# One product for delta's first factor, B and C; some elementwise work moved to GpSimd; a new job order

## The chip, the cores and the metric

The kernel runs on one core of one Trainium2 chip. The metric is the device time of one execution in microseconds (us). A core has five engines with queues of their own: TensorE (PE, matrix products and transposes; PEld is its weight load), VectorE (DVE), ScalarE (ACT), GpSimd (POOL) and SyncE (SP, which issues the DMAs here). Each works off its instructions in program order and waits on semaphores.

## The reference

A block of three parts on a stream x of 4 x 1024 tokens with 512 channels: a feed-forward layer with ternary weights, a selective state-space layer (Mamba), and the same feed-forward layer again.

```python
def step(h, inp):                       # N = 16 states per channel
    d_l, B_l, C_l, x_l = inp
    h = h * exp(d_l[:, :, None] * A) + (d_l * x_l)[:, :, None] * B_l[:, None, :]
    return h, einsum('ben,bn->be', h, C_l)

def ffn(x):                             # wu, wg, wd: ternary(W), 512 <-> 2048
    return (silu(x @ wu.T) * (x @ wg.T)) @ wd.T

def mamba(r):                           # E = 1024 channels inside
    rn = rmsnorm(r) * norm_w
    skip, x_in = rn @ W_skip, rn @ W_in
    x = silu(causal_conv4(x_in, conv_w) + conv_b)          # depthwise, 4 taps
    delta = softplus(x @ W_delta_1 @ W_delta_2 + b_delta_2) # 1024 -> 128 -> 1024
    y = scan(step, delta, x @ W_B, x @ W_C, x)
    return r + ((y + x * W_D) * silu(skip)) @ W_out

x = x + 0.5 * ffn(layernorm(x))
x = x + mamba(layernorm(x))
x = x + 0.5 * ffn(layernorm(x))
```

## The kernel before, in words

The 4096 tokens are cut into 16 chunks of 256. Everything is pipelined by hand over the chunks: while chunk i is scanned, chunk i+1 goes through the first feed-forward layer and the projections before the scan, and chunk i-1 through the output projection and the second feed-forward layer. The phases are "fill", "first", 14 times "loop", "last" and "drain".

A phase has 32 slots. Each slot holds one step of the scan (one of the 16 states, for one half of the 1024 channels) on all engines:

- POOL writes u times B into a ring of four buffers `h` (L647, 128x1024) and adds the state carried over (L651). It works three steps ahead of the transposes (`U_AHEAD`).
- ACT makes the decay exp(delta A) in PSUM (L880), two steps ahead.
- DVE runs the scan over the 256 tokens (L1164, two instructions for a step).
- PE transposes the states into PSUM (L1377, `states_T`, the last thing in its slot). It waits until DVE has added up the step before (`y_added`).
- DVE multiplies the transposed states by C and adds them up in `y` (L1190, `y_add`; L1187 for the first state of a half).

So in each slot DVE's `y_add` must be done before PE's transposes of that slot, and these before DVE's `y_add` of the next slot. PE and DVE can't drift apart by more than about a slot.

Between these stand the jobs, in the order of a table written out by hand, `LOOP_SLOTS` (L88): U and G are the up and gate products of the feed-forward layers for 256 hidden channels (U1, G1 first layer, U2, G2 second), DN the down products, T and Tp transposes of normalised rows, SK and IN the projections of the Mamba layer by quarters of the channels, D1 delta's first factor, BC the product for B and C, BT its transpose for B, D2_q delta's second factor, YT_q the transpose of y back, OM the output projection. ("OM_0", 0, 4) is parts 0 to 3 of a job. A job writes to one of four PSUM banks, and a later job waits until the other engines have used the bank's content (`bank_used`). The same table gives the slot in which ACT, DVE and POOL treat a result: a job that is not the last of its slot in that slot, the last one in the next.

What the change touches: `hidden_gate` (L1200, DVE: gate product times the activated up product, 16 in a chunk), `gated` (L1250, DVE: y + x D, and then times the skip gate `gz`), `conv` (L1222, DVE: three of the four taps, six instructions for a quarter), `delta_1` (L1443), `b_and_c` (L1450), `b_T` (L1467), and their readers on ACT (L934, L938, L981). Of `x_times_d` (L753, POOL), `mask_history` (L1215, DVE) and `mask_carry` (L1166, DVE) it moves only the slot. `first_state` (L653, POOL) stands in slot 6 of a chunk for the second half of the channels and waits for `mask_carry`, which DVE has in slot 8.

Of the kernel before, what the change touches and what calls it, by code (L numbers as in the profile page):

```python
# [21 lines left out]
P = 128  # L22
D, E, F, N, DD = 512, 1024, 2048, 16, 128
B, L = 4, 1024
TAPS = 4
TOK = B * L
CH = 256
# [5 lines left out]
CONV_STEPS = (TAPS - 1) * 2 - 1  # L33
# [23 lines left out]
def planes_of(s):  # L57
# [26 lines left out]
    ["D1", "BC"],  # L84
    ["BT", "D2_0", "D2_1"],
# [3 lines left out]
    ["T1_0", "T1_1", ("OM_0", 0, 4)],  # L89
    ["U1_0", "G1_0"],  # L90
    ["U1_1", "G1_1"],
    ["U1_2", "G1_2"],
    ["U1_3", "G1_3", "YT_2"],
    ["YT_3", "U1_4", "G1_4"],
    ["U1_5", ("OM_0", 4, 5), "G1_5", "U1_6"],
    [("OM_0", 5, 8), "G1_6"],
    [("DN1_0", 0, 3), ("OM_1", 0, 8)],
    ["U1_7", "G1_7"],
    [("DN1_1", 0, 1), ("DN1_0", 3, 9), ("DN1_1", 1, 2)],
    [("DN1_0", 9, 14)],  # L100
    ["T2_0", ("DN1_0", 14, 16), ("DN1_1", 2, 5)],
    [("DN1_1", 5, 12), ("SK_0", 0, 1), "T2_1"],
    [("DN1_1", 12, 16), ("SK_0", 1, 2), ("SK_1", 0, 2)],
    [("SK_2", 0, 2)],
    [("SK_3", 0, 1), "U2_0"],
    [("SK_3", 1, 2), "Tp_1"],
    ["Tp_0", "G2_0"],
    [("IN_2", 0, 2)],
    [("IN_3", 0, 2), ("IN_0", 0, 1), "U2_1"],
    ["YT_0", "YT_1", "G2_1", ("IN_0", 1, 2)],  # L110
    ["U2_2", "G2_2", ("IN_1", 0, 2)],
    ["U2_3", "G2_3", "U2_4"],
# [35 lines left out]
    ["D1"],  # L148
    ["BC", "D2_0", "D2_1"],
    ["BT", "D2_2", "D2_3"],  # L150
# [42 lines left out]
NEXT = {"T1_0", "T1_1", "DN1_0", "DN1_1", "Tp_0", "Tp_1", "IN_0", "IN_1", "IN_2", "IN_3", "D1", "BC", "BT", "D2_0", "D2_1", "D2_2", "D2_3"} | UG[1]  # L193
# [7 lines left out]
for _ph, _has in PHASES.items():  # L201
# [6 lines left out]
    assert set(ORDER[_ph]) == _has and len(SLOTS[_ph]) == STEPS  # L208
NBANK = 4
# [4 lines left out]
XD_0 = 2  # L214
XD_1 = 8
NEXT_LN = 29
MASK_1 = 8
MASK_0 = 24
MASK_H = 0
# [14 lines left out]
def step_of(ph, i, p):  # L234
# [61 lines left out]

def job_no(ph, i, name):
# [48 lines left out]
def macaron_kernel(nc, resid, norm_w, W_skip, W_in, conv_w, conv_b, W_delta_1, W_delta_2, b_delta_2, W_B, W_C,  # L346
# [10 lines left out]
    with ctx:  # L357
# [81 lines left out]
        y = sb("y", [P, TB, HE * P])  # L439

# [10 lines left out]
        wd1_loaded, wd2_loaded, wbc_loaded = sem("wd1_loaded"), sem("wd2_loaded"), sem("wbc_loaded")  # L451
# [57 lines left out]
        def _(sp):  # L509
# [98 lines left out]
        def _(pool):  # L608
# [118 lines left out]
            def add_edges(ph, i, half):  # L727
# [34 lines left out]
            def run(ph, i):  # L762
# [4 lines left out]
                for s in range(STEPS):  # L767
# [8 lines left out]
                    if after(ph, "OM_1", 0, s):  # L776
                        rstd(ph, i, "2")
                    for kind, p in hidden_units(ph, s):
                        hidden_low(ph, i, kind, p)
# [24 lines left out]
        def _(sc):  # L804
# [110 lines left out]
            def conv_in(ph, i, q):  # L915
# [673 lines left out]
```

## Time and profile before

| | us |
|---|---|
| median of 3 runs | 3043.34 (3043.31 to 3052.29) |
| the profiled execution | 3045.95 |
| its span, first to last instruction | 3044.2 |
| PE busy | 2796.4 (92%) |
| DVE busy | 2709.3 (89%) |
| POOL busy | 1993.6 (65%) |
| ACT busy | 1809.8 (59%) |

A busy time is the union of an engine's instructions. Matmuls overlap in their pipeline, so the pace of PE is read from the starts of successive ones, or from the chain of waits, whose pieces don't overlap. Of the waits of the engines, those count that end last before the chain goes on; most of ACT's and POOL's waits cost nothing.

### The profile page before, as it was taken

How to read it: one execution, taken by the hardware profiler on the slowest of the kernel's cores; microseconds unless marked ns; L12 is line 12 of the kernel's file. 1: busy time of each engine (PE TensorE's matmuls, PEld its weight loads, DVE VectorE, ACT ScalarE, POOL GpSimd, SP SyncE). 2: the span in 40 equal slices, each digit the busy share in tenths (PEclk: the TensorE clock that was granted, in tenths of full speed). 3: DMA queues.
4: the chain of work that ended last, by engine and by line, in shares of the span. 5: the costliest groups of instructions: out<-in, count | busy, mean ns of one | idle time of the engine just before them, and what ended most of it. 6: DMA issues, size and time to landing. Idle time of an engine off the chain costs nothing.

```text
span 3044.2 us, 53491 instructions
## 1 busy us (share of the span) xinstructions
PE 2796.4 (92%) x18791; PEld 2192.2 (72%) x18791; DVE 2709.3 (89%) x3613; ACT 1809.8 (59%) x4212; POOL 1993.6 (65%) x1875
## 2 busy tenths in 40 slices
PE   4777899999999999999999999999999999999888
PEld 3556677776877777787777768777777877777655
DVE  6359898999999999998999899999999989999992
ACT  6255656565565656556565655656565565656551
POOL 2165676757677675767777576776757677775761
PEclk9888899999999999999999999999999999999888
DMA  6010101001010100101010010101001010100100
GB/s 252 28 32 18 32 22 36 18 22 43 15 39 22 36 18 22 43 17 37 21 36 18 22 43 15 39 22 36 18 22 43 17 38 22 36 18 22 35 29 8
DMA packets 53313, 99.88 MB, mean 33 GB/s; under 512 B 7804, under 2 KB 9144, under 8 KB 52536
## 3 DMA queue, kind: packets, MB, share of 16 engines
q1 hardware_dynamic: 53048, 96.45, 10.1%
q8 instruction: 153, 2.51, 0.3%
q14 instruction: 112, 0.92, 0.1%
HBM read 87.78 MB, written 8.65 MB: 32 GB/s over the span
## 4 chain that ended last, share of the span: by engine, by line
PE 64%; DVE 20%; issue 6%; ACT 3%; POOL 1%; DVEq 0%; ACTq 0%; POOLq 0%
PE ps L1415 17%; PE ps L1426 14%; PE ps L1438 11%; PE ps L1377 10%; DVE h L1164 8%; PE ps L1491 6%; DVE y L1190 4%; DVE xc L1233 2%; PE ps L1447 2%; PE ps L1454 2%; PE ps L1464 2%; DVE act L1206 1%; DVE act L1198 1%; DVE xw L1256 1%; ACT ps L880 1%
## 5 line engine op out<-in xcount | busy, mean ns | idle before, releaser
L647 POOL TENSOR_TENSOR h<-u,bb 128x1024 f32<-128x1024 f32 x512 | 1222.1, 2387 | 305.5 <-PE ps L1377 298.4
L880 ACT ACTIVATE ps<-delta,a_neg 128x255 f32<-128x255 f32 x2048 | 882.4, 466 | 664.1 <-DVE h L1164 662.2
L1164 DVE TENSOR_TENSOR_SCAN h<-ps,h 128x512 f32<-128x512 f32 x1024 | 1191.8, 1205 | 33.3 <-POOL h L651 17.6
L1190 DVE SCALAR_TENSOR_TENSOR y<-ps,ccur,y 128x512 f32<-128x512 f32 x960 | 670.3, 739 | 46.9 <-PE ps L1377 45.9
L1377 PE MATMUL ps<-ident,h 128*128 128x128 f32 x4096 | 564.1, 280 | 97.4 <-DVE y L1190 93.2
L1377 PEld LDWEIGHTS ps<-ident,h 128*128 128x128 f32 x4096 | 475.7, 144 | 183.8 <-issue 80.4
L1415 PE MATMUL ps<-xh,q_gate 128*128 128x256 f16 x2048 | 462.4, 273 | 37.5 <-DVE act L1198 22.6
L1415 PE MATMUL ps<-xh,q_up 128*128 128x256 f16 x2048 | 466.6, 275 | 15.9 <-DVE xl L1103 12.9
L1415 PE MATMUL ps<-xl,q_up 128*128 128x256 f16 x2048 | 466.7, 275 | 0.0
L1415 PE MATMUL ps<-xl,q_gate 128*128 128x256 f16 x2048 | 462.1, 273 | 0.0
L742 POOL TENSOR_TENSOR hl<-act,hh 128x512 f16<-128x512 f32 x256 | 300.9, 1178 | 233.5 <-ACT hh L905 233.5
L1426 PE MATMUL ps<-q_down,hh 128*128 128x512 fp8e4 x1024 | 388.9, 380 | 3.1 <-issue 2.8
L1426 PE MATMUL ps<-q_down,hl 128*128 128x512 fp8e4 x1024 | 388.7, 380 | 0.0
L900 ACT ACTIVATE act<-ps,tanh_sc 128x512 f32<-128x512 f32 x256 | 173.3, 677 | 192.6 <-PE ps L1415 125.7
L1415 PEld LDWEIGHTS ps<-xh,q_gate 128*128 128x128 fp8e4 x2048 | 200.6, 98 | 77.2 <-issue 53.5
L1198 DVE SCALAR_TENSOR_TENSOR act<-act,ps 128x512 f32<-128x512 f32 x256 | 173.0, 676 | 82.8 <-ACT act L900 82.8
L1438 PE MATMUL ps<-xrT,w_in 128*128 128x256 f32 x1024 | 234.6, 383 | 1.1 <-ACT xrT L911 1.1
L1415 PEld LDWEIGHTS ps<-xh,q_up 128*128 128x128 fp8e4 x2048 | 201.5, 98 | 47.4 <-issue 19.4
L1491 PE MATMUL ps<-w_out,gz 128*128 128x512 f32 x512 | 234.7, 603 | 0.7 <-DVE gz L1259 0.7
L1438 PE MATMUL ps<-xrT,w_skip 128*128 128x256 f32 x1024 | 233.9, 379 | 0.0
L1415 PEld LDWEIGHTS ps<-xl,q_gate 128*128 128x128 fp8e4 x2048 | 200.6, 98 | 35.1 <-issue 9.3
L1415 PEld LDWEIGHTS ps<-xl,q_up 128*128 128x128 fp8e4 x2048 | 201.7, 98 | 31.6
(133 smaller groups left out, 3449.4 us busy)
## 6 DMA issues: line engine op xcount, KB each, us to landing
bb<-b_scratch SPq DMA_DIRECT2D x224, 256.0 KB, 3.2
xs<-in_L_attn_resid_dram SPq DMA_DIRECT2D x17, 512.0 KB, 3.8
out_dram<-xs SPq DMA_DIRECT2D x16, 512.0 KB, 4.3
wraw<-in_L_ffn_W_up_dram SPq DMA_DIRECT2D x4, 1024.0 KB, 8.9
wraw<-in_L_ffn_W_gate_dram SPq DMA_DIRECT2D x4, 1024.0 KB, 13.1
wraw<-in_L_ffn_W_down_dram SPq DMA_DIRECT2D x4, 1024.0 KB, 14.2
w_in<-in_L_attn_W_in_dram SPq DMA_DIRECT2D x1, 2048.0 KB, 21.6
w_skip<-in_L_attn_W_skip_dram SPq DMA_DIRECT2D x1, 2048.0 KB, 8.8
```

Source lines behind the costliest of these rows:

```text
L647: pl.tensor_tensor(h[:, s % RING, :, :], u[:, :, :], bb[:, planes_of(s) % 2, s % PLANES:s % PLANES + 1, :].broadcast_to([P, HE, CH]), ALU. ...
L742: pl.tensor_tensor(hl[:, 2 * p:2 * p + 2, :], act[:, p % ACTS, :].rearrange("q (f t) -> q f t", f=2), hh[:, 2 * p:2 * p + 2, :], ALU.subtr ...
L880: ins = ac.activation(abar[r][:, e, 1:], delta[:, k, 1:], ACT.Exp, scale=a_neg[:, k, n:n + 1])
L900: ac.activation(act[:, p % ACTS, :], pp, ACT.Tanh, scale=tanh_sc[:, 0:1]).then_inc(tanh_ready, 1)
L1164: v.tensor_tensor_scan(hr, abar[r].rearrange("p e t -> p (e t)"), hr, 0.0, ALU.mult, ALU.add).then_inc(scanned, 1)
L1190: ins = v.scalar_tensor_tensor(out=yy, in0=hT[:, t, :], scalar=cc, in1=yy, op0=ALU.mult, op1=ALU.add)
L1198: v.scalar_tensor_tensor(out=a, in0=a, scalar=1.0, in1=pp, op0=ALU.add, op1=ALU.mult).then_inc(bank_used[bk], 1)
L1377: ins = te.transpose(hT[:, t, e * P:(e + 1) * P], h[:, s % RING, e, t * P:(t + 1) * P], ident[:, :])
L1415: ins = te.matmul(pp[:, f * CH:(f + 1) * CH], w[:, d, col:col + P], part[:, d, :], start=(d == 0 and part is xh), stop=(d == DB - 1 and pa ...
L1426: ins = te.matmul(pp, part[:, f, t * P:(t + 1) * P], q_down[:, f, :], start=(f == 0 and part is hh), stop=(f == FB - 1 and part is hl))
L1438: ins = te.matmul(pp[:, e * CH:(e + 1) * CH], w[:, d, col:col + P], xrT[:, d, :], start=(d == 0), stop=(d == DB - 1))
L1491: ins = te.matmul(pp, gz[:, e, t * P:(t + 1) * P], w_out[:, e, :], start=(e == 0), stop=(e == EB - 1))
```

## The change

Four things change together.

1. `w_d1` and `w_bc` become one tensor `w_db` of 160 columns. One job DB multiplies the transposed activations (as the stationary operand) by all 160 columns, token by token, in place of D1 and BC. ACT copies the result to `dbn`. A job DT transposes delta's factor (two full transposes) and B (two of 16 rows) back; ACT copies both out. D2 reads the factor from there.
2. The multiplication by the skip gate (second instruction of `gated`) goes to POOL, four in a chunk.
3. For one pair of hidden channels in each feed-forward layer (pair 6 of the first, 4 of the second), ACT copies the gate product to SBUF and POOL multiplies; `hl` of that pair is one slot later.
4. The farthest tap of the convolution for the second half of the channels: ACT writes tap times input to SBUF, and POOL adds it (128x4x253) behind the edges.

And the table of jobs is new, with the slots of five single instructions.

```diff
+POOL_PAIRS = {1: [6], 2: [4]}
+FAR_ON_POOL = [1]
-XD_0 = 2
-XD_1 = 8
+XD_0 = 3
+XD_1 = 11
-MASK_0 = 24
-MASK_H = 0
+MASK_0 = 27
+MASK_H = 1
 LOOP_SLOTS = [
-    ["T1_0", "T1_1", ("OM_0", 0, 4)],
+    ["T1_0", "T1_1", ("OM_0", 0, 4), "U1_0"],
...
-    [("DN2_0", 5, 8), "D1", "G2_5"],
-    ["D2_0", "BC", ("DN2_0", 8, 9)],
+    ["G2_5", "DB", ("DN2_0", 2, 5)],
+    ["DT", ("DN2_0", 5, 8)],
...
# POOL
+            def hidden_gate(ph, i, kind, p):
+                g = gate_no(ph, i, kind, p)
...
+                pl.tensor_tensor(act[:, p % ACTS, :], act[:, p % ACTS, :], gates[:, g % GATES, :],
+                                 ALU.mult).then_inc(hidden_gated, 1)
+            def gated(ph, i, q):
...
+                pl.tensor_tensor(gz[:, qb, :], xw[:, qb, :], gz[:, qb, :], ALU.mult).then_inc(z_ready, 1)
# POOL, add_edges
+                if far_on_pool(ph, half):
+                    xx = xc[:, half * HE:(half + 1) * HE, TAPS - 1:]
+                    pl.tensor_tensor(xx, xx, far_tap[half][:, :, TAPS - 1:], ALU.add).then_inc(far_added, 1)
# ACT
+            def gate_copy(ph, i, kind, p):
...
+                ac.activation(gates[:, g % GATES, :], pp, ACT.Copy, scale=HID_SCALE).then_inc(bank_used[bk], 1)
+                        ac.activation(far_tap[q // 2][:, b % HE, TAPS - 1:], pp[:, e * CH:(e + 1) * CH - TAPS + 1],
+                                      ACT.Copy, scale=cw[:, b:b + 1])
+            def delta_b_rows(ph, i):
+                bk, pp = ready(ph, i, "DT")
+                ac.activation(d1T, pp[:, 0:CH].rearrange("p (t n) -> p t n", t=TB), ACT.Copy)
# DVE, conv and gated
-                for tap in range(TAPS - 1):
+                for tap in range(begin, TAPS - 1):
-                v.tensor_tensor(gz[:, qb, :], yx, gz[:, qb, :], ALU.mult).then_inc(z_ready, 1)
# PE
-                for e in range(EB):
-                    ins = te.matmul(pp[:, 0:CH], w_d1[:, e, :], xc[:, e, :], start=(e == 0), stop=(e == EB - 1))
+            def delta_b_c(ph, i):
...
+                        ins = te.matmul(pp[:, t * DB_COLS:(t + 1) * DB_COLS], xc[:, e, t * P:(t + 1) * P], w_db[:, e, :],
+                                        start=(e == 0), stop=(e == EB - 1))
+            def delta_b_T(ph, i):
...
+                for t in range(TB):
+                    te.transpose(pp[:, t * P:(t + 1) * P], dbn[:, t, 0:DD], ident[:, :])
```

How the rows move on PE, in slots 25 and 26 of the loop. Before (L1415 the end of G2_5, L1377 the transposes of the states, L1464 D2_0, L1454 BC, L1426 a part of DN2_0; D1 stands ahead of G2_5):

```order
L1415 MATMUL ps<-xh,q_gate 128x256
L1415 MATMUL ps<-xl,q_gate 128x256
L1377 MATMUL ps<-ident,h 128x128 x8
L1464 MATMUL ps<-d,w_d 128x256 x2
L1454 MATMUL ps<-w_bc,xc 128x32 x16
L1426 MATMUL ps<-q_down,hh 128x512
L1426 MATMUL ps<-q_down,hl 128x512
```

After (L1508 the end of G2_5, L1541 DB, L1519 three parts of DN2_0, L1470 the transposes of the states, L1550 and L1552 DT):

```order
L1508 MATMUL ps<-xh,q_gate 128x256
L1508 MATMUL ps<-xl,q_gate 128x256
L1541 MATMUL ps<-w_db,xc 128x160 x16
L1519 MATMUL ps<-q_down,hh 128x512
L1519 MATMUL ps<-q_down,hl 128x512
L1519 MATMUL ps<-q_down,hh 128x512
L1519 MATMUL ps<-q_down,hl 128x512
L1519 MATMUL ps<-q_down,hh 128x512
L1519 MATMUL ps<-q_down,hl 128x512
L1470 MATMUL ps<-ident,h 128x128 x8
L1550 MATMUL ps<-ident,dbn 128x128 x2
L1552 MATMUL ps<-ident,dbn 16x128 x2
```

The product for B and C now stands ahead of D2, DT (with B's transpose, which stood in slot 30) stands in slot 26, and D2_0 follows only in slot 27.

On DVE, in slots 21 and 22. Before (L1198 and L1206 up and gate product, L1187 the first `y_add` of a half, L1242 the convolution's activation, L1256 and L1259 `gated`, L1164 scan, L1190 `y_add`, L1233 taps of the convolution):

```order
L1198 SCALAR_TENSOR_TENSOR act<-act,ps 128x512
L1187 TENSOR_SCALAR y<-ps,ccur 128x512 x2
L1242 SCALAR_TENSOR_TENSOR xc<-tmp,xc 128x1024
L1256 TENSOR_TENSOR xw<-ps,xw 128x512
L1259 TENSOR_TENSOR gz<-xw,gz 128x512
L1256 TENSOR_TENSOR xw<-ps,xw 128x512
L1259 TENSOR_TENSOR gz<-xw,gz 128x512
L1206 SCALAR_TENSOR_TENSOR act<-ps,act 128x512
L1164 SCALAR_TENSOR_TENSOR h<-ps,h 128x512 x2
L1190 SCALAR_TENSOR_TENSOR y<-ps,ccur,y 128x512 x2
L1233 SCALAR_TENSOR_TENSOR xc<-ps,vcol,xc 128x253 x2
L1233 SCALAR_TENSOR_TENSOR xc<-ps,vcol,xc 128x254 x2
```

On DVE, in slots 20 and 21, after (L1327 taps of the convolution, L1291 and L1299 up and gate product, L1350 y + x D, L1257 scan, L1280 the first `y_add` of a half, L1336 the convolution's activation):

```order
L1327 SCALAR_TENSOR_TENSOR xc<-ps,vcol,xc 128x254 x2
L1327 SCALAR_TENSOR_TENSOR xc<-ps,vcol,xc 128x255 x2
L1291 SCALAR_TENSOR_TENSOR act<-act,ps 128x512
L1350 TENSOR_TENSOR xw<-ps,xw 128x512
L1257 SCALAR_TENSOR_TENSOR h<-ps,h 128x512 x2
L1280 TENSOR_SCALAR y<-ps,ccur 128x512 x2
L1327 SCALAR_TENSOR_TENSOR xc<-ps,vcol,xc 128x253 x2
L1327 SCALAR_TENSOR_TENSOR xc<-ps,vcol,xc 128x254 x2
L1327 SCALAR_TENSOR_TENSOR xc<-ps,vcol,xc 128x255 x2
L1336 SCALAR_TENSOR_TENSOR xc<-tmp,xc 128x1024
L1350 TENSOR_TENSOR xw<-ps,xw 128x512
L1299 SCALAR_TENSOR_TENSOR act<-ps,act 128x512
```

L1259 is gone; the quarters of the second half have lost their taps 128x253 and end in slot 20; the next quarter's taps now stand behind the first `y_add`, and y + x D is spread over two slots.

## Rows read from the trace of the kernel before

**Rows 1.** The page, busy time of the engines: us, share, instructions.
```profile
PE 2796.4 (92%) x18791; PEld 2192.2 (72%) x18791; DVE 2709.3 (89%) x3613; ACT 1809.8 (59%) x4212; POOL 1993.6 (65%) x1875
```

**Rows 2.** Windows: window, us, busy PE, PEld, DVE, ACT, POOL (instructions), clock, DMA share, GB/s.
```profile
400.00:2700.00 2300.00, 2209.66 (x15055) 1738.27 (x15054) 2155.95 (x2891) 1421.74 (x3366) 1600.17 (x1503) 1.00 0.09 28
1507.00:1685.00 178.00, 170.99 (x1168) 134.29 (x1166) 167.12 (x225) 110.09 (x261) 124.33 (x117) 1.00 0.10 28
```

**Rows 3.** Timeline of DVE, one scan and the same one a chunk later.
```profile
1506.18 2.32 DVE L1164 TENSOR_TENSOR_SCAN h<-ps,h 128x512 f32<-128x512 f32 x2
...
1683.48 2.33 DVE L1164 TENSOR_TENSOR_SCAN h<-ps,h 128x512 f32<-128x512 f32 x2
```

**Rows 4.** Waits of PE, 1507 to 1685 us: total us, times, longest.
```profile
PE ps L1377 <- DVE y L1190: 2.8, 2, 1.9
PE ps L1415 <- DVE act L1198: 1.6, 1, 1.6
PE ps L1415 <- DVE xl L1103: 0.7, 1, 0.7
PE ps L1482 <- issue: 0.6, 1, 0.6
PE ps L1415 <- DVE xc L1233: 0.6, 1, 0.6
PE ps L1415 <- DVE xw L1256: 0.5, 1, 0.5
```

**Rows 5.** The chain of waits: start, us of the piece, matmul records in it.
```profile
1536.21 3.45 PE ps L1447 x16
...
1541.41 0.87 PE ps L1377 x8
...
1543.15 3.49 PE ps L1454 x32
...
1567.92 0.22 PE ps L1472 x2
```

**Rows 6.** Timeline of DVE: start, us, instruction.
```profile
1501.51 4.75 DVE L1233 SCALAR_TENSOR_TENSOR xc<-ps,vcol,xc 128x253 f32<-128x253 f32 x12
...
1511.66 0.68 DVE L1256 TENSOR_TENSOR xw<-ps,xw 128x512 f32<-128x512 f32 x1
1512.38 0.69 DVE L1259 TENSOR_TENSOR gz<-xw,gz 128x512 f32<-128x512 f32 x1
1512.99 0.68 DVE L1256 TENSOR_TENSOR xw<-ps,xw 128x512 f32<-128x512 f32 x1
...
1514.32 0.68 DVE L1206 SCALAR_TENSOR_TENSOR act<-ps,act 128x512 f32<-128x512 f32 x1
1514.92 2.33 DVE L1164 TENSOR_TENSOR_SCAN h<-ps,h 128x512 f32<-128x512 f32 x2
```

**Rows 7.** Groups of POOL and ACT by form, 400 to 2700 us: busy, mean ns.
```profile
L742 POOL TENSOR_TENSOR hl<-act,hh 128x512 f16<-128x512 f32 x207 | 239.3, 1159 | 159.1 <-ACT hh L905 159.1
L708 POOL TENSOR_TENSOR delta<-delta,tmp 128x1024 f32<-128x1024 f32 x13 | 30.6, 2356 | 0.0
L923 ACT ACTIVATE xc<-ps,vcol 128x256 f32<-128x256 f32 x104 | 53.0, 560 | 70.3 <-PE ps L1438 70.3
```

**Rows 8.** Waits of POOL and of DVE for it, 1507 to 1685 us.
```profile
POOL h L647 <- PE ps L1377: 17.9, 11, 5.1
POOL xc L736 <- DVE xc L1233: 8.2, 2, 4.2
POOL a L658 <- issue: 7.9, 1, 7.9
```
```profile
DVE h L1164 <- POOL h L651: 1.2, 1, 1.2
```

**Rows 9.** Two instructions, timeline: DVE's mask of the history, POOL's beside it.
```profile
1576.69 1.16 DVE L1219 TENSOR_TENSOR hist<-hist,keep 128x24 int32<-128x24 int32 x1
```
```profile
1575.46 2.35 POOL L647 TENSOR_TENSOR h<-u,bb 128x1024 f32<-128x1024 f32 x1
```

More of the change, by code:

```diff
@@ L32 @@
 HE = EB // 2
-CONV_STEPS = (TAPS - 1) * 2 - 1
+DB_COLS = DD + 2 * N
 STEPS = 2 * N
@@ L83 @@
     [],
-    ["D1", "BC"],
-    ["BT", "D2_0", "D2_1"],
+    ["DB"],
+    ["DT", "D2_0", "D2_1"],
     ["D2_2", "D2_3"], [], [], [], [], [], [], [], [], [], [],
@@ L147 @@
     [],
-    ["D1"],
-    ["BC", "D2_0", "D2_1"],
-    ["BT", "D2_2", "D2_3"],
+    ["DB"],
+    ["DT", "D2_0", "D2_1"],
+    ["D2_2", "D2_3"],
     [],
@@ L192 @@
 THIS = {"SK_0", "SK_1", "SK_2", "SK_3", "YT_0", "YT_1"}
-NEXT = {"T1_0", "T1_1", "DN1_0", "DN1_1", "Tp_0", "Tp_1", "IN_0", "IN_1", "IN_2", "IN_3", "D1", "BC", "BT", "D2_0", "D2_1", "D2_2", "D2_3"} | UG[1]
+NEXT = {"T1_0", "T1_1", "DN1_0", "DN1_1", "Tp_0", "Tp_1", "IN_0", "IN_1", "IN_2", "IN_3", "DB", "DT", "D2_0", "D2_1", "D2_2", "D2_3"} | UG[1]
 PHASES = {"fill": NEXT, "first": THIS | NEXT, "loop": PREV | THIS | NEXT, "last": PREV | THIS, "drain": PREV}
@@ L294, with far_on_pool, conv_steps, far_no @@
 JOBS = {(ph, p): [n for n in ORDER[ph] if BANK_OF[ph][n] == p] for ph in PHASES for p in range(NBANK)}
+def far_on_pool(ph, half):
+    return ph != "fill" and half in FAR_ON_POOL
+def conv_steps(ph, i, turns):
+    full = (TAPS - 1) * 2 - 1
+    if ph == "fill":
+        return full * turns
+    each = [full - 2 * far_on_pool(ph, 1 - k // 2) for k in range(QT)]
+    return QT * full + i * sum(each) + sum(each[:turns])
+def far_no(i, half):
+    return len(FAR_ON_POOL) * i + FAR_ON_POOL.index(half)
 def job_no(ph, i, name):
@@ L308, in job_no, with phase_of @@
     return p, before
+def phase_of(c):
+    return "first" if c == 0 else ("last" if c == NCH - 1 else "loop")
 def ffn_run(ph, i, kind):
@@ L317, in ffn_run, with gate_no @@
     return 2 * i + (kind - 1) if ph == "loop" else (2 * NCH - 2 if ph == "last" else 2 * NCH - 1)
+def gate_no(ph, i, kind, p):
+    done = {"fill": (0, 0), "first": (1, 0), "loop": (i + kind, i - 1), "last": (NCH, NCH - 2), "drain": (NCH, NCH - 1)}[ph]
+    return sum(len(POOL_PAIRS[k]) * n for k, n in zip((1, 2), done)) + POOL_PAIRS[kind].index(p)
 def ln_run(ph, i, kind):
@@ L777, in run @@
                         rstd(ph, i, "2")
+                    for q in range(QT):
+                        if after(ph, f"YT_{q}", 0, s):
+                            gated(ph, i, q)
+                    for kind, p in hidden_units(ph, s - 1):
+                        if p in POOL_PAIRS[kind]:
+                            hidden_low(ph, i, kind, p)
                     for kind, p in hidden_units(ph, s):
-                        hidden_low(ph, i, kind, p)
+                        if p in POOL_PAIRS[kind]:
+                            hidden_gate(ph, i, kind, p)
+                        else:
+                            hidden_low(ph, i, kind, p)
                     if after(ph, "DN1_1", 0, s):
```

158 lines of the change are left out of this document (79 added, 79 removed), and 24 rows, old and new, of tables (BEFORE, LOOP_SLOTS).

## The prediction, made before the changed kernel was timed

> **What bounds the kernel now.** I read the page's busy times first: PE 92% and DVE 89% of the span, POOL 65%, ACT 59% [rows 1]. Two engines are nearly full, so a saving on one of them alone is worth little unless it is on the path. The windows say that this is steady: from 400 to 2700 us PE is busy 96% of the time and DVE 94%, at the full granted clock [rows 2]. Next comes the length of a chunk, from a scan and the same scan a chunk later: 1683.48 - 1506.18 = 177.3 us [rows 3]. The loop has 14 such chunks, 2482 of the 3044 us of span. Last the waits of PE inside this chunk: six groups, 2.8 + 1.6 + 0.7 + 0.6 + 0.6 + 0.5 = 6.8 us, nearly all of them for DVE [rows 4]. So a chunk is 170.5 us in which PE issues without a pause, and 6.8 us in which it waits for DVE, which itself is busy for 167.1 us [rows 2]. PE's work is the bound; where DVE has more in a stretch of slots than PE, the surplus is added as a wait, because `y_add` couples them within a slot. ACT and POOL wait much of the time (POOL 17.9 us of a chunk for PE alone [rows 8]).
>
> **PE's part of the change.** It removes D1 (3.45 us), BC (3.49) and BT (0.22) [rows 5], together 7.16 us. D1's 8 matmuls are 16 records at 0.216 us for 256 columns; BC's 16 are 32 records at 0.109, for only 32 columns, and the transposes pass 128 columns in 0.87/8 = 0.109 too [rows 5]. BC is thus paced by something other than its columns, and 128 columns are as cheap as 32. DB has 32 records of 160 columns. No row shows 160 columns. From below the price is BC's, 0.109 each, 3.5 us; from above D1's, 0.216, 6.9 us. I take the straight line between 128 and 256 columns, 0.109 + 32 x 0.107/128 = 0.136, since 128 is the nearest row: 32 x 0.136 = 4.35 us. DT adds four transposes: two for the factor and two for B, each at 0.11 as in BT, 0.44 us in all; D2 keeps its price. So 7.16 becomes 4.8, a saving of 2.4 us a chunk. The ends are 3.5 + 0.44 (saving 3.2) and 6.9 + 0.44 (0.2 dearer).
>
> The Trainium skill, "TensorE: Matmul & The Clock Gate", section "Back-to-back issue gap", gives N/2.4 + 2.5 ns for one matmul of N columns, under which even 160 columns would hide behind the weight load and DB would cost its lower end. The trace doesn't agree for this data type: 256 columns pace at 216 ns in D1, where the formula has 109. So the line between the rows stands.
>
> The new chain DB, ACT copy, DT, ACT copy, D2_0 could be a wait. Between DB and DT stand DN2_0's three parts and the transposes of the states (0.87 us), between DT and D2_0 the same again. An ACT copy of 256 columns takes 0.56 us [rows 7], and two follow DT. I cost it at nothing. It is tight in slot 26, which is a short one on PE (2.8 us of jobs and transposes): if ACT comes there only after its decays, D2_0 waits, up to 1 us. In exchange B is stored four slots earlier than now.
>
> **DVE's part.** Starts of successive instructions give the price with what they hold up. L1256 with L1259 takes 1512.99 - 1511.66 = 1.33 us; alone it is 0.6 as L1206 (1514.92 - 1514.32) [rows 6]. Four L1259 go: 4 x 0.73 = 2.9 us. Two L1206 go: 1.2. Of the convolution 12 taps take 1506.18 - 1501.51 = 4.67 us [rows 3, 6], 0.39 each, and four go: 1.6. In all DVE loses 5.7 us, 167.1 to 161.4.
>
> **What hides the added work.** POOL gets six products of 128x512: 1.16 us each by L742 (the same count of elements, f16 out), 1.18 by half of L708 [rows 7], 7.1 us; and one addition of 128x1012, 2.35 us. That is 9.4 us, 124.3 [rows 2] to 133.8. Against a chunk of some 171 us it is 78%. Where it stands counts more. The two skip gates of slot 5 (2.4 us) precede `first_state` of slot 6, where POOL idles 7.9 us a chunk for DVE's `mask_carry` in slot 8 [rows 8]: covered. The addition behind the edges stands in slot 20 after a wait of about 4.2 us for the convolution [rows 8], and POOL is then two slots ahead of the scan that needs it: covered, though its cover shrinks. The gate of pair 6 stands in slot 9, when POOL is catching up after the mask. There DVE already waits 1.2 us for POOL [rows 8]. But XD_1 (1.9 us) moves out of that stretch to slot 11, and OM_0's use (about 1.5 us of DVE work) moves in behind the mask in slot 8, which gives POOL time: that wait should go, not grow. ACT gets some 4 us: two gate copies (0.6 each), four taps (0.5 each [rows 7]), a second copy for the factor. The two taps delay `conv_begun` by 1 us in each of two quarters; in slot 20 DVE reaches the quarter IN_3 after that of IN_2, so about a microsecond may be waited there, where DVE has room.
>
> The Trainium skill, "GPSIMD Engine Reference", section "Key points", speaks against the move: POOL shares its SBUF interfaces with VectorE and contends with DVE instructions that have two SBUF inputs, and elementwise work is about twice as slow on it. The trace agrees: DVE's mask of 24 elements takes 1.16 us and ends just when POOL's 2.35 us product beside it ends, at 1577.8 [rows 9]. Yet the instruction moved off DVE most often, L1259, has two SBUF inputs itself, so four exposed ones go; taps and gates read PSUM. Left exposed are the two activations of the convolution and the masks. POOL being busy 8% more of the time, I put nothing in the sum for it.
>
> **The waits that go.** I summed the jobs of each slot by these prices, with 0.87 for PE's transposes and 3.56 for DVE's scan and `y_add`. Slots 20 to 24: before 33.4 us on PE and 37.6 on DVE; after 32.2 and 33.7. That is the place of the waits for L1198, L1233, L1256 and of the 0.6 at L1482 (3.3 us together [rows 4]): DVE is 4 us over there now, and hardly later. The wait for xl, 0.7, stands at slot 0 to 1; the mask of the history (1.1 us) leaves slot 0 ahead of it: it goes too, but U1_0 is now drawn into slot 0 and meets xl earlier, so I count half. The 2.8 us for L1190 stand at the end of the chunk, where PE's slots 28 and 29 (8 us each) let DVE run dry and the softplus on POOL, the decays and the scan then follow one another. Slot 29 gets shorter (8.2 to 6.5) and slot 30 longer; D2_3 stays in slot 28, so I keep the 2.8. The waits fall from 6.8 to 6.8 - 3.3 - 0.35 = 3.15; new small ones (ACT in slots 20 and 26) I put at 0.4, so 3.55.
>
> **The sum.** 2.4 on PE and 3.25 of waits are 5.65 us a chunk, 14 x 5.65 = 79. The 2 products of fill and first save 2 x 2.4, on the path if PE is, 4.8; for DVE's relief in the phases at the ends I take 1. Together 85 us from the profiled execution, 3045.95 to 2961. The median of the runs lies 2.6 below the profiled one: 2958.
>
> **The rivals.**
>
> (A) The forecast: PE remains the bound, half of its waits go. 2958. For it: DVE is the releaser of nearly all of them, and it loses more than PE. Own range 2930 to 2985.
>
> (B) Only PE's saving counts. The waits stay as large, moved to other slots, because DVE and PE are coupled slot by slot and the new order has very uneven slots on PE (9.9 us in slot 10 and 2.2 in slot 11, 10.0 in 20). 16 x 2.4 = 38 us: 3005. For it: the order before is about as uneven and has 6.8. Against: DVE's sum falls 10 us under the length of a chunk, so it can catch up sooner.
>
> (C) All waits of PE go: 14 x (2.4 + 6.8) + 5 = 134 us: 2909. Against: the chain of softplus and decays at the end of a chunk is not shortened.
>
> (D) Slower. POOL becomes the last link: it is at 88% in the slots from the end of one chunk into the next, and its instructions stand in a fixed order, some blocked on DVE (the mask, the convolution). If each of the added 9.4 us delayed a scan, the chunk would go by the chain POOL, DVE, PE: 177.3 - 5.7 (DVE's) + 9.4 = 181.0, 52 us more over the loop: 3095. It decides from the point where more than 5.7 of the 9.4 us are not covered. Against: POOL's waits before the places named are 7.9 and 4.2 us.
>
> (E) The copies, the gate on POOL and the transposes put back what the product saves, as PE pays the upper price (0.2 dearer) and new waits take the place of the old: within 0.3%, 3043. Against: 160 columns are far nearer to 128 than to 256.
>
> **How the numbers follow.** A 0.66, B 0.17, C 0.06, D 0.06, E 0.05. A run of this kernel can tell some 0.3%, 9 us, from no change (the three runs spread by 9 us). A, B and C are faster: 0.89; same 0.05; slower 0.06. The range takes A and reaches over most of B, and two thirds of the way to C, where the lower price of DB (14 x 0.8 = 11 us) also lies: 2925 to 3008.
>
> **What would show it.** In the profile after: a chunk of about 171.7 us; DB as 32 records at 0.136 and 4.35 us in the chain, DT 0.44; DVE busy about 161 us and PE about 168 of a chunk; PE's waits for up product, xw and xc gone and only the one at the end of the chunk left, some 3 us; POOL near 134 us a chunk, with its wait in `first_state` cut from 7.9 to about 5; DVE's wait for POOL under 1.2. Wrong would be: DB at 0.2 us a record; PE waits of 6 us or more in other places (B); DVE waiting for POOL's h by several us a chunk (D); D2_0 waiting for ACT.

## The result, and the profile after

| | before | after |
|---|---|---|
| median, us | 3044.32 | 2992.8 (2991.49 to 2995.87) |
| profiled execution's span | 3044.2 | 2994.1 |
| one chunk (mean of the steady state before: 177.6) | 177.3 | 174.1 |
| PE's waits in a chunk | 6.8 | 4.75 |

The 3044.32 is the kernel before, timed again beside the changed one. The ratio is 0.9827, with a 95% interval of 0.9808 to 0.9845: 51.5 us faster. The forecast was 85 us (2958). Its direction and the two engines were right; of the size some 60% came.

The busy times on the page after, which answer to [rows 1]:

```profile
PE 2773.2 (93%) x18567; PEld 2180.6 (73%) x18567; DVE 2607.0 (87%) x3457; ACT 1844.8 (62%) x4304; POOL 2140.9 (72%) x1986
```

DVE has lost 102 us, PE 23, POOL has got 147 and ACT 35. The window of steady state, columns as in [rows 2]:

```profile
400.00:2650.00 2250.00, 2186.96 (x14849) 1726.78 (x14848) 2064.56 (x2754) 1448.34 (x3440) 1716.35 (x1587) 0.99 0.09 28
```

Over 174.1 us DVE is busy for 2064.56/2250 x 174.1 = 159.8 us (161 forecast) and POOL for 132.8 (134). Two chunks, by the first `y_add` of each half (timeline of DVE; start, us), give the length; the first and the third row are of slot 5, the others of slot 21:

```profile
1401.61 1.41 DVE L1280 TENSOR_SCALAR y<-ps,ccur 128x512 f32<-128x512 f32 x2 [0.57 <-PE ps L1571]
...
1485.07 1.41 DVE L1280 TENSOR_SCALAR y<-ps,ccur 128x512 f32<-128x512 f32 x2
...
1575.58 1.41 DVE L1280 TENSOR_SCALAR y<-ps,ccur 128x512 f32<-128x512 f32 x2 [0.57 <-PE ps L1571]
1659.30 1.41 DVE L1280 TENSOR_SCALAR y<-ps,ccur 128x512 f32<-128x512 f32 x2
```

1575.58 - 1401.61 = 173.97 and 1659.30 - 1485.07 = 174.23. The waits of PE in one chunk after, for comparison with [rows 4]:

```profile
PE ps L1470 <- DVE y L1283: 3.3, 4, 2.1
PE ps L1571 <- DVE y L1283: 1.4, 1, 1.4
```

The waits for the up product, the taps, xw and xl are gone. What is left is `y_add`, and a wait ahead of YT_2. Where the waits stand is read from the timeline of PE (start, us; idle before and its releaser). Before, in slots 31, 4 and 18:

```profile
1573.10 1.22 PE L1377 MATMUL ps<-ident,h 128*128 128x128 f32 x8 [1.93 <-DVE y L1190]
...
1598.57 0.63 PE L1482 MATMUL ps<-ident,y 128*128 128x128 f32 x4 [0.64 <-issue]
...
1670.69 1.23 PE L1377 MATMUL ps<-ident,h 128*128 128x128 f32 x8 [0.90 <-DVE y L1190]
```

After, in the same slots:

```profile
1545.57 1.22 PE L1470 MATMUL ps<-ident,h 128*128 128x128 f32 x8 [2.12 <-DVE y L1283]
...
1571.68 0.63 PE L1571 MATMUL ps<-ident,y 128*128 128x128 f32 x4 [1.43 <-DVE y L1283]
...
1643.24 1.23 PE L1470 MATMUL ps<-ident,h 128*128 128x128 f32 x8 [0.68 <-DVE y L1283]
```

The other two waits after are of 0.24 and 0.25 us, in slots 22 and 24. So PE without its waits takes 174.1 - 4.75 = 169.35 us a chunk, and 168.1 was forecast. The difference is not DB. The chain of waits shows both (start, us, matmul records; [rows 5] has it before):

```profile
1509.76 4.61 PE ps L1541 x32
...
1516.54 0.22 PE ps L1550 x2
1516.76 0.22 PE ps L1552 x2
...
1546.79 1.70 PE ps L1492 x8
1548.50 4.29 PE ps L1580 x8
```

DB takes 4.45 from its start at 1509.76 to that of the next job at 1514.21, 0.139 a record, and DT 0.44. But the last two pieces, T1 and OM_0 at the start of a chunk, take twice and 1.25 times what they should: eight transposes pace at 0.87 us [rows 5], and eight records of OM take 3.44 us in a later piece of the same chain. The windows show why:

```profile
1543.00:1546.50 3.50, 1.38 (x12) 0.99 (x10) 3.46 (x5) 3.37 (x12) 3.23 (x4) 1.00 0.13 34
1546.50:1550.00 3.50, 3.50 (x14) 2.47 (x13) 3.35 (x5) 2.52 (x6) 2.78 (x4) 0.52 0.00 0
```

The granted clock is 0.52 in the second window, so it stands at the lower of TensorE's two levels (1.2 GHz) for nearly all of it. PE's 2.12 us of idle time end at 1545.57; the clock is still full from 1545.5 to 1546.4, while the transposes of the states pass, 0.50 from 1546.8 to 1549.8, and 0.99 from 1550 to 1553. It is so in each chunk, as the groups by form over the steady state say (busy, mean ns):

```profile
L1580 PE MATMUL ps<-w_out,gz 128*128 128x512 f32 x416 | 197.1, 618 | 0.0
...
L1492 PE MATMUL ps<-ident,xn 128*128 128x128 f32 x204 | 39.5, 346 | 0.0
```

Before, the same counts of records were busy for 187.1 us (592 ns on the mean) and 28.5 us (273 ns): 21 us less over 13 chunks, 1.6 a chunk.

### The profile page after: what moved, and what is told of

Same layout as the page of the kernel before. It is cut to its first block, busy times and chain, and to the rows that moved or that the text cites. A ratio compares the mean times of both kernels' runs of the same rounds, so it can differ in the third digit from the quotient of the medians.

```text
span 2994.1 us, 53240 instructions
## 1 busy us (share of the span) xinstructions
PE 2773.2 (93%) x18567; PEld 2180.6 (73%) x18567; DVE 2607.0 (87%) x3457; ACT 1844.8 (62%) x4304; POOL 2140.9 (72%) x1986
## 4 chain that ended last, share of the span: by engine, by line
PE 60%; DVE 19%; issue 7%; ACT 7%; POOL 1%; DVEq 0%; ACTq 0%; POOLq 0%
PE ps L1508 15%; PE ps L1519 14%; PE ps L1470 10%; PE ps L1580 8%; DVE h L1257 7%; PE ps L1531 7%; DVE y L1283 4%; DVE xc L1327 3%; PE ps L1541 2%; ACT ps L950 2%; PE ps L1561 2%; DVE act L1291 2%; PE ps L1492 1%; DVE xc L1336 1%; DVE act L1299 1%
## 5 line engine op out<-in xcount | busy, mean ns | idle before, releaser
L1257 DVE TENSOR_TENSOR_SCAN h<-ps,h 128x512 f32<-128x512 f32 x1024 | 1192.3, 1207 | 11.2 <-ACT ps L950 11.0
L1470 PE MATMUL ps<-ident,h 128*128 128x128 f32 x4096 | 564.0, 280 | 100.0 <-DVE y L1283 96.0
L1470 PEld LDWEIGHTS ps<-ident,h 128*128 128x128 f32 x4096 | 475.6, 143 | 182.3 <-issue 93.3
L1508 PE MATMUL ps<-xh,q_up 128*128 128x256 f16 x2048 | 465.9, 274 | 7.0 <-DVE xl L1196 4.1
L1508 PE MATMUL ps<-xl,q_up 128*128 128x256 f16 x2048 | 465.8, 274 | 0.0
L1508 PE MATMUL ps<-xh,q_gate 128*128 128x256 f16 x2048 | 461.8, 273 | 0.0
L1508 PE MATMUL ps<-xl,q_gate 128*128 128x256 f16 x2048 | 461.7, 273 | 0.0
L1519 PE MATMUL ps<-q_down,hh 128*128 128x512 fp8e4 x1024 | 388.1, 379 | 2.9 <-issue 2.8
L1519 PE MATMUL ps<-q_down,hl 128*128 128x512 fp8e4 x1024 | 388.1, 379 | 0.0
L1291 DVE SCALAR_TENSOR_TENSOR act<-act,ps 128x512 f32<-128x512 f32 x256 | 173.6, 678 | 118.5 <-ACT act L970 118.4
L1580 PE MATMUL ps<-w_out,gz 128*128 128x512 f32 x512 | 247.6, 629 | 2.1 <-POOL gz L812 2.1
L1508 PEld LDWEIGHTS ps<-xh,q_up 128*128 128x128 fp8e4 x2048 | 201.6, 98 | 36.4 <-issue 11.2
L1508 PEld LDWEIGHTS ps<-xl,q_up 128*128 128x128 fp8e4 x2048 | 201.6, 98 | 33.6 <-issue 4.6
L1508 PEld LDWEIGHTS ps<-xl,q_gate 128*128 128x128 fp8e4 x2048 | 200.6, 98 | 30.8 <-issue 4.6
L1508 PEld LDWEIGHTS ps<-xh,q_gate 128*128 128x128 fp8e4 x2048 | 200.6, 98 | 27.1 <-issue 3.5
## 6 DMA issues: line engine op xcount, KB each, us to landing
wraw<-in_L_ffn_W_down_dram SPq DMA_DIRECT2D x4, 1024.0 KB, 14.2
```

The source lines that it names most:

```text
L1257: v.tensor_tensor_scan(hr, abar[r].rearrange("p e t -> p (e t)"), hr, 0.0, ALU.mult, ALU.add).then_inc(scanned, 1)
L1291: v.scalar_tensor_tensor(out=a, in0=a, scalar=1.0, in1=pp, op0=ALU.add, op1=ALU.mult).then_inc(bank_used[bk], 1)
L1470: ins = te.transpose(hT[:, t, e * P:(e + 1) * P], h[:, s % RING, e, t * P:(t + 1) * P], ident[:, :])
L1508: ins = te.matmul(pp[:, f * CH:(f + 1) * CH], w[:, d, col:col + P], part[:, d, :], start=(d == 0 and part is xh), stop=(d == DB - 1 and pa ...
L1519: ins = te.matmul(pp, part[:, f, t * P:(t + 1) * P], q_down[:, f, :], start=(f == 0 and part is hh), stop=(f == FB - 1 and part is hl))
L1580: ins = te.matmul(pp, gz[:, e, t * P:(t + 1) * P], w_out[:, e, :], start=(e == 0), stop=(e == EB - 1))
```

## The experiments

Each batch was timed beside the kernel before (3045 to 3046 us). "Changed" is the changed kernel at 2992.8; its own four executions lie between 2991.5 and 2995.9, so differences from it of 4 us and less are not told from none. The chunk is the mean of 25 or 26 lengths in the steady state (177.6 before, 174.1 changed), from one first `y_add` of a half to the same one a chunk later. PE's waits are those of the window from 400 to 2600 us, over the number of chunks in it (by this count 6.9 before and 4.8 changed).

| run | us | ratio to before | chunk | PE's waits in it |
|---|---|---|---|---|
| old order, product alone | 3016.5 | 0.9901 (0.9886 to 0.9916) | 175.7 | 6.8 |
| old order, product and all moves | 3078.6 | 1.0104 (1.0090 to 1.0118) | 180.3 | 9.8 |
| the same, one piece of DN2_0 later | 3014.5 | 0.9901 (0.9888 to 0.9915) | 175.8 | 6.3 |
| new order, product alone | 3053.0 | 1.0022 (1.0013 to 1.0031) | 178.0 | 9.1 |
| changed, skip gate on DVE | 3059.8 | 1.0052 (1.0038 to 1.0066) | 178.6 | 9.4 |
| changed, two of four skip gates on DVE | 3002.1 | 0.9859 (0.9842 to 0.9875) | 174.6 | 5.9 |
| changed, no pairs on POOL | 2996.6 | 0.9841 (0.9828 to 0.9854) | 174.1 | 5.0 |
| changed, far tap on DVE | 2993.3 | 0.9833 (0.9819 to 0.9846) | 174.0 | 4.8 |
| changed, neither (skip gate alone) | 2996.4 | 0.9835 (0.9822 to 0.9849) | 174.1 | 5.1 |
| changed, PE's wait filled | 2978.6 | 0.9778 (0.9765 to 0.9791) | 172.8 | 3.1 |
| changed, work in the last slot | 2975.0 | 0.9765 (0.9752 to 0.9778) | 172.8 | 5.0 |
| the same with the old slots 0 to 5 | 2969.9 | 0.9748 (0.9735 to 0.9762) | 172.4 | 3.7 |

### Is the slower clock a real cost?

```diff
                         if (ph, name[:2]) != ("fill", "T1"):
                             job(ph, i, name, lo, hi)
...
+                    if ph == "loop" and s == STEPS - 1 and i < NCH - 2:
+                        bk, before = job_no("loop", i + 1, "U1_0")
+                        need(pe, bank_used[bk], before)
+                        for _ in range(16):
+                            te.transpose(bank[bk][:, 0:P], ident[:, :], ident[:, :])
```

> The changed kernel, with 16 transposes of the identity added on PE in slot 31 of 13 of the 14 loop chunks, into the bank that U1_0 takes next; they compute nothing that is used. They fill 1.75 of the some 2.3 us in which PE stands idle ahead of the last transposes of a chunk. Theory 1: the granted clock falls to 0.52 for some 3.3 us after that idle time (T1 1.70 us in place of 0.87, OM_0 4.29 in place of 3.44), which costs 1.65 us a chunk; with PE occupied it does not fall, so 13 x 1.65 = 21 us less: 2971. Rival: what follows the idle time is bound by DVE and ACT anyway, and the slower clock is hidden, or it falls whatever stands there: 2993, or a little more for the added work.

2978.6: 14.2 us less by adding 208 instructions. The clock stays full in this place, as the groups by form show for the steady state:

```profile
L1580 PE MATMUL ps<-w_out,gz 128*128 128x512 f32 x416 | 187.1, 592 | 0.0
```

The clock's price is real, the rival falls. Of the 21 us by which the slow matmuls were longer 14 came back by the medians (18 by the two profiled executions, 2995.87 and 2977.51). Why not all is not shown; in this run PE waits 0.22 us a chunk for xl, which it does not in the changed kernel.

### The order and the moves, each without the other

The product alone in the old order: the table of jobs as before, with these lines and without BT in slot 30, and the three moves undone.

```diff
-    [("DN2_0", 5, 8), "D1", "G2_5"],
-    ["D2_0", "BC", ("DN2_0", 8, 9)],
-    ["D2_1", "U2_6"],
+    [("DN2_0", 5, 8), "DB", "G2_5"],
+    ["DT", ("DN2_0", 8, 9)],
+    ["D2_0", "D2_1", "U2_6"],
```

> The kernel before with the one product alone, in the old order. PE's saving is 7.16 - 4.45 (DB as measured in the profile after) - 0.44 = 2.3 us a chunk. If PE's work is the bound: 16 x 2.3 = 36 us less than before, 3008. Rival: PE's waits for DVE grow by as much, since DVE is busy for 167 of 177 us: 3030 to 3044.

3016.5, 29 of the 36 us of PE's saving. PE's waits stay 6.8 us a chunk. The rest is about the clock again: it fell behind the last slot in 5 of the 12 chunks from 400 to 2600 us, where T1's transposes are busy for 31.2 us against 27.5 before and the output projection for 175.2 against 172.7. That is 6.2 us, or 0.5 us a chunk. So the product pays nearly in full, and by itself.

The new order with the product, moves undone (`POOL_PAIRS = {1: [], 2: []}`, `FAR_ON_POOL = []`, and `gated` on DVE as in the kernel before):

> The new order of jobs and the one product, with all three moves undone: skip gate, pairs and far tap are back on DVE (5.7 us a chunk more on it). Theory 1 (the moves unload DVE, which is still waited for): DVE is again the later one in slots 20 to 24, at least 2 us a chunk, 30 us or more slower than 2993, so 3020 to 3045. Rival (the moves brought nothing, POOL and ACT hand the time back): within 5 us of 2993.

3053.0: with DVE loaded as before, the new order is 36.5 us slower than the old one, and the kernel slower than before. PE waits 9.1 us a chunk. The theory holds, a little beyond its range.

All moves with the product in the old order:

> The old order of jobs (DB where D1 was, DT where D2_0 was, D2_0 first in slot 27; XD and mask slots as before) with the one product and all three moves. Theory 1 has half of the gain from the product and DVE's relief alone: 3005 to 3015, the order giving some 15. Rival (the order is the change's core, and the moves need it): 3035 or more. Second rival (the new order hurts through the clock and the wait for YT_2, both absent here): under 2993, near 2985.

3078.6, far slower than before. The trace names the place (PE's waits, 12 chunks):

```profile
PE ps L1519 <- POOL hl L790: 43.8, 12, 3.7
PE ps L1470 <- DVE y L1283: 39.5, 37, 2.2
```

L1519 is a down product; it waits 3.65 us in each chunk, in slot 26, for `hl` of pair 4, which the move to POOL makes one slot later, while (DN2_0, 8, 9) has to have it there. The new order has that piece in slot 28. So this run was partly a fault of my table, and I moved the piece:

```diff
-    ["DT", ("DN2_0", 8, 9)],
+    ["DT"],
-    ["G2_6", "D2_2", "U2_7", "D2_3", "G2_7"],
+    ["G2_6", "D2_2", ("DN2_0", 8, 9), "U2_7", "D2_3", "G2_7"],
```

> As the run with the old order, all moves and the product (3079), but the piece (DN2_0, 8, 9) stands in slot 28 and not in 26. In that run PE waited 3.65 us a chunk there for POOL's hl of pair 4, which comes a slot later since its gate product is on POOL. Theory: that wait alone made the old order slow; without it 14 x 3.65 = 51 us less, 3028, and more if the chunk's end gets looser. Rival: the wait only moves to another piece or place, and the moves are worth nothing in the old order: 3060 or more.

3014.5: 64 us for one piece, where the wait itself is 14 x 3.65 = 51. The windows of the run before, behind this wait, show what comes on top: the clock is at the lower level when PE starts again, here in the second stretch.

```profile
1554.00:1557.30 3.30, 0.00 (x0) 0.00 (x0) 2.75 (x3) 2.37 (x8) 3.22 (x4) 1.00 0.02 7
1557.30:1560.50 3.20, 3.15 (x12) 2.61 (x13) 1.14 (x2) 0.36 (x1) 1.27 (x2) 0.50 0.22 74
```

The records of D2 that follow are busy for 57.1 us in 12 chunks there and for 51.4 in 13 with the piece moved: 0.8 us a chunk, 11 us over the 14. So both, the wait and the clock, make up 62 of the 64 us. The run is also within 2 us of the product alone: in the old order the three moves, with this piece in slot 28, are worth nothing that can be told, although DVE's busy time falls from 166.4 to 161.7 us a chunk. What the piece's new slot does without the moves was not run. Added to the product, the order brings -36 us, the moves bring 2, and both together bring 24.

### Which move?

The changed kernel with one move undone each (the constants emptied, or the product of `gated` put back behind DVE's addition):

> The changed kernel with the skip gate back on DVE (four products of 0.69 us a chunk, 2.9 us with what they hold up), the rest as changed. All three moves together were worth 60 us in this order (3053 without, 2993 with). Theory 1: DVE's load decides, and each move is worth its share of the 5.7 us a chunk: 2.9/5.7 x 60 = 31, so 3024. Rival (only the place counts: two of the gates stand in slot 5 beside YT_2 and YT_3 and two in 20 and 21, where DVE is late): more than 40 us, 3033 or above.

> The changed kernel with the gate products of all 16 pairs on DVE (1.2 us a chunk more), the rest as changed. By share of load: 1.2/5.7 x 60 = 13 us, 3005. Rival: the long way of a pair (ACT copy, POOL product, ACT, POOL; DVE's wait for ACT's tanh is 5.7 us a chunk after, 3.2 before) costs as much as it frees: 2985 to 2995.

> The changed kernel with the far tap back on DVE (four instructions, 1.6 us a chunk), the rest as changed. By share of load: 1.6/5.7 x 60 = 17 us, 3010. Rival: the new waits that the far tap brings (DVE for ACT's hist copy 1.2 us, for the tanh behind POOL's addition 1.1 us a chunk) eat it: 2990 to 2997.

3059.8, 2996.6 and 2993.3. The share of load as a rule is wrong in all three: the skip gate is worth 67 us, the pairs 4 (which is not clear of the spread), the far tap nothing. Nor do the moves add up: with all three undone the time was 3053.0, so with the gate on DVE the other two moves make the kernel 7 us slower. The far tap's own new waits are in the changed kernel's list of DVE (steady state, 13 chunks, 1.2 us each). The pairs add to its waits for ACT's tanh: 65 of them here, 72.0 us, and 52 without pairs, 63.5 us.

```profile
DVE act L1291 <- ACT act L970: 72.0, 65, 2.0
...
DVE xc L1327 <- ACT hist L1016: 15.6, 13, 1.2
```

> The changed kernel with far tap and pairs back on DVE, so product, new order and the skip gate on POOL alone. With each of the two undone alone the time was 2993 and 2997, with the gate undone 3060. Theory (the skip gate is all of the moves' worth in this order): 2993 to 3003. Rival (far tap and pairs stand in for one another, DVE's load being just short enough with either): 3010 or more.

2996.4, as the theory had it: the two other moves do not stand in for one another. The gate by itself is worth 3053.0 - 2996.4 = 57 us in this order.

Where the skip gate acts is seen in the timeline of PE with the gate on DVE, slot 22 (start, us; idle before and its releaser):

```profile
1519.86 0.27 PE L1507 MATMUL ps<-xh,q_gate 128*128 128x256 f16 x1 [1.61 <-DVE xc L1324]
...
1522.54 3.72 PE L1530 MATMUL ps<-xrT,w_in 128*128 128x256 f32 x16 [0.77 <-DVE xw L1347]
...
1527.44 1.23 PE L1469 MATMUL ps<-ident,h 128*128 128x128 f32 x8 [1.18 <-DVE y L1280]
```

G2_2 wants the bank in which IN_0 stood, and DVE's taps of IN_0 come late; IN_1 wants that of YT_1. Of these 3.6 us the changed kernel has 0.2, ahead of the transposes of the states.

DVE is late there by more than its own two gate products. Its timeline in that run (start, us; L1350 is the gate, L1333 the convolution's activation):

```profile
1511.77 2.06 DVE L1350 TENSOR_TENSOR gz<-xw,gz 128x512 f32<-128x512 f32 x1
...
1519.64 2.24 DVE L1333 SCALAR_TENSOR_TENSOR xc<-tmp,xc 128x1024 f32<-128x1024 f32 x1
...
1522.52 0.69 DVE L1350 TENSOR_TENSOR gz<-xw,gz 128x512 f32<-128x512 f32 x1
```

and POOL beside it:

```profile
1510.95 2.34 POOL L775 TENSOR_TENSOR xc<-xc,ln 128x1012 f32<-128x1012 f32 x1
...
1518.46 2.35 POOL L683 TENSOR_TENSOR h<-u,bb 128x1024 f32<-128x1024 f32 x1 [2.13 <-PE ps L1469]
```

The first gate begins while POOL's addition runs and takes 2.06 us, where the second, with no POOL instruction beside it, takes 0.69. The activation begins while POOL's product runs and takes 2.24 us; in the changed kernel, where POOL's product is over before it, it takes 1.22. So of DVE's delay in slots 20 to 22 some 2.4 us is this lengthening, and 1.4 us is the two gates at 0.69. All four gates of a chunk take 1.49, 1.61, 2.06 and 0.69 us here, 5.9 together. In the kernel before, the same four take 0.75 to 0.82 us in slot 5 and 0.69 in the other place, 3.0 together, and in the new order without any move again 5.8. So the new order puts DVE's gates beside POOL's instructions. How much of its loss without the gate's move comes from that no run separates.

A last run put only the gates of YT_2 and YT_3 (slot 5) back on DVE:

```diff
+                if q >= 2:
+                    need(ve, bank_used[bk], job_no(ph, i, f"YT_{q}")[1] + 1)
+                    v.tensor_tensor(gz[:, qb, :], yx, gz[:, qb, :], ALU.mult).then_inc(z_ready, 1)
```

> The changed kernel with the skip gates of YT_2 and YT_3 (slot 5) back on DVE and those of YT_0 and YT_1 (slots 20 and 21) still on POOL: half of the 2.9 us a chunk that the four cost DVE. All four back cost 67 us. Theory (place decides: in slots 20 and 21 a gate on DVE holds back the taps of IN_0 and the use of YT_1, whose banks G2_2 and IN_1 wait for, 1.6 + 0.8 + 1.2 us a chunk in that run's trace; in slot 5 PE waits no longer for it than the 0.7 us that two products are behind y_add): 2995 to 3010. Rival (DVE's load decides, wherever): 67/2, 3020 to 3035.

3002.1: those two are worth 9 us in the changed kernel, and with them on DVE the two of slots 20 and 21 another 58. The 9 understate what the first two cost in waits: PE's waits grew by 1.2 us a chunk, some 16 us, but the clock fell in only two chunks of the steady state, where the changed kernel loses up to 1.6 us in each. By PE's waits the two in slot 5 cost 1.2 us a chunk and the two in slots 20 and 21 3.4. DVE's added time is nearly the same: 1.49 + 1.61 = 3.1 us for the first two, 3.8 for the others with the longer activation. So the place decides more than the load. That the 3.8 us would be 1.4 without POOL beside them, and the price then smaller, was not run.

### Real work in the wait

```diff
-    [("DN2_0", 11, 16), ("DN2_1", 11, 16)],
-    [],
+    [("DN2_0", 11, 16), ("DN2_1", 11, 12)],
+    [("DN2_1", 12, 16)],
...
-    EARLY[_ph] = {n for jobs in SLOTS[_ph] for n, lo, hi in jobs[:-1] if hi == PARTS.get(n, 1)}
+    EARLY[_ph] = {n for jobs in SLOTS[_ph] for n, lo, hi in jobs[:-1] if hi == PARTS.get(n, 1)} | {n for n, lo, hi in SLOTS[_ph][-1]}
```

DN2_1 is used by DVE in slot 31 for it, behind `y_add`.

> The changed kernel with the last four parts of DN2_1 in slot 31 in place of slot 30, and its use by DVE behind the y_add of that slot in place of ahead of it (all of the computation is kept). PE's wait at the chunk's end (2.1 us) is partly filled with real work, and y_add comes 0.75 us earlier. Theory 1 (wait and falling clock are both real costs): 0.75 + 1.65 us a chunk, 14 x 2.4 = 34 us less than 2993: 2960. Rival: the end of a chunk is bound by ACT's softplus and decays, so PE's work moved there only fills, and the gain is the clock alone, as with the added transposes: 2975 to 2980. Second rival: T1_1 or OM_0 now wait for the bank: 2985 or more.

2975.0. The clock stays full. Between theory and rival the time is the rival's: the wait of 2.1 is 1.3 us, and a new one of 1.0 stands at U1_0 for xl, where the changed kernel has none:

```profile
1536.08 1.22 PE L1470 MATMUL ps<-ident,h 128*128 128x128 f32 x8 [1.32 <-DVE y L1283]
1542.62 0.27 PE L1508 MATMUL ps<-xh,q_up 128*128 128x256 f16 x1 [1.00 <-DVE xl L1196]
```

> As the run before, and slots 0 to 5 as in the kernel before (U1_0 in slot 1, U1_3 with G1_3 ahead of YT_2 in slot 4). Theory 1: the 1.4 us a chunk that PE waits for y_add ahead of YT_2 since U1_3 is gone from there shrinks to the 0.6 of before: 14 x 0.8 = 11 us less than the run before, 2950. Rival (U1_0 waits for xl in slot 1 as before, 0.7, or DVE is waited for in slots 1 to 4 instead): no gain, or up to 10 us slower.

2969.9, the fastest of all, with the whole computation kept: 23 us under the changed kernel. The wait ahead of YT_2 is 0.64 again, that for xl is gone, and one of 0.5 for xw has come. PE's waits fell by 1.3 us a chunk, yet the chunk by 0.3 only: PE was busy for 0.8 us a chunk longer with the same work, which no run explains. Of the 11 us expected, 5 came.

## Why the prediction was right in direction and too high in size

- **What bounds the kernel** (PE's work plus its waits for DVE): right. In every run with the product the chunk, without PE's waits, without the longer matmuls at the slow clock (0 to 2.1 us) and without the added transposes, is 167 to 169 us; 168.1 was forecast.
- **PE's part**: 2.4 us a chunk forecast; by DB's 4.45 and DT's 0.44 it is 2.3. The straight line gave 0.136 a record, 0.139 was measured. By the formula for a single matmul in the Trainium skill, "TensorE: Matmul & The Clock Gate", section "Back-to-back issue gap", an estimate for 160 columns is 160/2.4 + 2.5 = 69 ns; the trace has 139, twice that. Alone the product brought 29 us where its 16 x 2.3 are 36.
- **DVE's part**: 5.7 us forecast, 6.4 measured (166.2 to 159.8). The history mask, which I had left out of this sum, went from 1.16 us to 0.16 and is more than the surplus.
- **What hides the added work**: right. POOL's wait in `first_state` fell from 7.9 to 4.5 us, DVE's wait for POOL's `h` is gone, and D2_0 waits for no copy. The microsecond for `conv_begun` in slot 20 came (1.2) and the run without the far tap on POOL, where it is absent, is no faster. Nothing for the contention of POOL with DVE was right here: the convolution's activation has 1.29 us on the mean before and 1.28 after. It would not have been right elsewhere: the same instruction has 1.61 us in the old order with all moves, and 1.80 with the gate on DVE.
- **The waits that go**: this step failed. It said 6.8 to 3.55, and 4.75 were left. Some waits stand elsewhere than the prediction had them. The 0.6 at L1482 is ahead of YT_2 in slot 4 and not in slots 20 to 24; the relief summed up there did nothing for it, and it grew to 1.4, because the new slot 4 has no U1_3 to cover it (with U1_3 back it is 0.64). The 0.5 for L1256 is in slot 5, and went all the same. The 2.8 for L1190 are 1.93 in slot 31 and 0.90 in slot 18, not all at the chunk's end; after, they are 2.12 and 0.68, the same 2.8 by luck. The wait for xl went whole (half was counted as staying), and the new small ones are 0.49 (0.4 forecast).
- **The sum** took the full clock as given, since it was full before but for two short falls in the steady state [rows 2]. The slow matmuls are 1.6 us a chunk, of which filling the wait gave back 14 to 18 us in all. With 14 x 1.2 = 17 us for the waits it makes 31 to 35 us, and 33 were missing.
- **The reason for the gain**, "DVE loses 5.7 us, so it catches up", was too coarse. In the old order nearly the same relief brought 2 us. Two skip gates do most of the work, and only in the new order, which without them is slower than the old: there they would take 3.8 us of DVE's time with POOL beside them, and not 1.4. Which part of the gain is the place and which is this is not separated.

## What to carry to other kernels

In a pipeline of fixed order, price a move by the wait that it shortens at its place, not by the load that it takes from an engine: look up whose buffer the moved instruction holds back, who asks for it next, and what POOL runs beside it, since an instruction of DVE with two SBUF inputs can take two to three times as long there (0.69 and 2.06 us). Change order and placement together, since each alone may cost, and check every consumer of a result that comes a slot later. And where an engine with a throttled clock runs out of work at a fixed point of a loop, look at its granted clock behind that point; real work moved there, or even empty work, can pay.

## What the runs showed of the hardware

The clock fell behind an idle time of PE of 2.12 us at the end of each chunk of the changed kernel, and cost 1.6 us. It isn't the length of that wait alone. With 1.93 us in the same place (the kernel before) it never fell there in the steady state, and with 1.32 and 0.36 us (work in the last slot, the wait filled) neither. With 2.11 us it fell in all 13 chunks of the steady state in the runs without pairs, without the far tap and with the skip gate alone, but behind this wait in 2 of 13 in the new order with the product alone and in the run with two gates on DVE, and in 4 of 12 with all gates there. With 2.15 us, in the old order, it fell in 6 of 13 with the product alone and in every second chunk with all moves and the piece moved. It was also down behind the 3.65 us of the run with all moves. What decides besides the length stays open.

DVE's mask of 24 elements with two SBUF inputs took 1.16 us while POOL's 128x1024 product ran beside it [rows 9] and 0.16 one slot later in the changed kernel:

```profile
L1312 DVE TENSOR_TENSOR hist<-hist,keep x10: 157/158/161, 1031.1 to 2598.1; 128x24 int32<-128x24 int32 x10
```

It follows what POOL does beside it and not the slot or the moves. In the three other runs in the old order it has 1.17 us on the mean, and in all runs in the new order 0.16 but one: with the old slots 0 to 5 it stands in slot 1 too, meets POOL's product again, and takes 0.79 us, to the product's end (1543.14 by POOL's row, 1543.18 by DVE's):

```profile
1542.39 0.79 DVE L1312 TENSOR_TENSOR hist<-hist,keep 128x24 int32<-128x24 int32 x1
```
```profile
1540.78 2.36 POOL L683 TENSOR_TENSOR h<-u,bb 128x1024 f32<-128x1024 f32 x1 [0.20 <-POOL u L798]
```

The skip gate on DVE (128x512, two SBUF inputs) took 0.69 us with POOL idle and 1.49 to 2.06 where POOL's products or its addition were under way when it began, but 0.75 to 0.82 in slot 5 of the kernel before, where it began just before POOL's product or 0.3 us before its end. POOL's product is longer too where a gate is under way as it begins: 2.82 us in place of 2.36.
